# Graph network kernel: dot attention's edge one-hots made during propagation instead of in its own slot loop

## Time and profile before

| | |
|---|---|
| median of 3 runs | 1626.44 us (1622.48 to 1628.04) |
| the profiled execution | 1627.73 us, span 1625.9 us |
| propagation | 324.6 to 859 us |
| slot loop of graph attention | 995 to 1210 us |
| slot loop of dot attention | 1249 to 1524 us |
| busy share of the span: PE, DVE, ACT, POOL | 76%, 77%, 34%, 23% |

### The profile page before, as it was taken

The page is one execution under the profiler, slowest core; times in us unless marked ns, Lnnn a source line. Parts: engine busy times, 40 slices in busy tenths (PEclk is TensorE's granted clock), DMA queues, the critical chain, the costliest instruction groups (busy, mean ns, idle before and its releaser), DMA issues. The chain is left out here.

```text
span 1625.9 us, 44876 instructions
## 1 busy us (share of the span) xinstructions
PE 1237.4 (76%) x18543; PEld 1174.0 (72%) x18544; DVE 1259.8 (77%) x2302; ACT 546.2 (34%) x1096; POOL 373.9 (23%) x211
## 2 busy tenths in 40 slices
PE   4767777399999999999994004888856888888468
PEld 3356767399899999999993004787755887888368
DVE  7888888766566565665667998999988999999733
ACT  0047777400000000000002873333335777777311
POOL 1400000000000000000001012888862665656300
PEclk6858777699999999999997556999997999999789
DMA  0012222375475565654563683555513444543293
GB/s 10 0 46 109 105 103 109 109 249 190 151 240 204 161 196 194 213 194 164 203 213 110 225 298 123 204 201 189 200 68 117 144 159 149 164 146 122 96 343 101
DMA packets 74936, 256.85 MB, mean 158 GB/s; under 512 B 17999, under 2 KB 19576, under 8 KB 74732
## 3 DMA queue, kind: packets, MB, share of 16 engines
q1 hardware_dynamic: 59996, 211.70, 38.6%
q10 hardware_dynamic: 14400, 40.97, 6.5%
q0 software_dynamic: 336, 1.20, 0.3%
HBM read 168.15 MB, written 85.68 MB: 156 GB/s over the span
## 5 line engine op out<-in xcount | busy, mean ns | idle before, releaser
L1248 PE MATMUL psum<-work,count 128*128 128x192 f16 x6250 | 521.4, 247 | 30.7 <-issue 30.7
L1248 PEld LDWEIGHTS psum<-work,count 128*128 128x128 f16 x6250 | 519.7, 98 | 32.5 <-issue 31.8
L1171 DVE SCALAR_TENSOR_TENSOR work<-psum,small,work 128x96 f32<-128x96 f32 x250 | 79.5, 318 | 177.4 <-PE psum L1248 177.3
L1585 PE MATMUL psum<-count 128*128 128x98 f16 x625 | 113.1, 209 | 134.5 <-DVE count L1632 98.2
L1852 PE MATMUL psum<-count 128*128 128x100 f16 (+1 forms) x1875 | 181.4, 207 | 44.5 <-DVE count L1941 30.7
L1852 PEld LDWEIGHTS psum<-count 128*128 128x128 f16 x1875 | 162.7, 98 | 55.3 <-issue 36.0
L929 ACT ACTIVATE work<-work 128x1248 f32<-128x1248 f32 (+1 forms) x6 | 7.2, 1203 | 576.9 <-DVE work L912 576.8
L1917 POOL TENSOR_TENSOR count<-count 128x1000 bf16<-128x1000 f32 (+1 forms) x75 | 160.8, 2143 | 122.0 <-ACT count L1901 122.0
L1624 POOL TENSOR_TENSOR count<-count 128x970 bf16<-128x970 f32 (+1 forms) x75 | 166.7, 2236 | 91.2 <-ACT count L1617 91.2
L1853 PE MATMUL psum<-count 128*128 128x100 f16 (+1 forms) x1875 | 180.8, 207 | 0.0
L1853 PEld LDWEIGHTS psum<-count 128*128 128x128 f16 x1875 | 164.4, 98 | 0.0
(11 more groups left out here) (286 smaller groups left out, 2695.7 us busy)
## 6 DMA issues: line engine op xcount, KB each, us to landing
x<-bucket_rows_by_src SPq DMA_DIRECT2D x100, 400.0 KB, 4.6
onehots_by_src<-x ACTq DMA_DIRECT2D x100, 400.0 KB, 4.3
count<-bucket_rows_by_dst SPq DMA_DIRECT2D x50, 800.0 KB, 4.4
count<-onehots_by_src SPq DMA_DIRECT2D x50, 800.0 KB, 4.3
count_f<-count SPq DMA_DIRECT2D x25, 800.0 KB, 6.8
count<-count_turned SPq DMA_DIRECT2D x25, 800.0 KB, 5.8
count<-count_f SPq DMA_DIRECT2D x17, 800.0 KB, 4.3
count_turned<-x SPq DMA_DIRECT2D x25, 416.0 KB, 2.4
```

The source lines that it names most:

```text
L1248: last = nc.tensor.matmul(bank[i % BANKS], count16[:, j, i * P:(i + 1) * P], y[par][:, j, :], start=(j == 0), stop=(j == TILES - 1))
L1585: nc.tensor.matmul(ps[:, at:at + GW], node_hot[SRC][t % 2][:, s, :], high[:, s, :], start=True, stop=False, skip_group_check=True)
```

## The change

The edge one-hots of dot attention too are made in propagation and stored as a third set of 25 rows in hot_by_src. The 50 node rows are cut into 200 quarters of 800 columns with four buffers, the 25 edge rows into 125 fifths of 640 columns with two buffers. DVE compares one quarter after each of the tiles 1 to 20 of a step, and behind five quarters of every eight an edge fifth. The ids for the edge compares come from ids_dram in five chunks of five src tiles, 20 bytes for each partition and dst tile, into two buffers; two are loaded ahead of the first quarter, one each behind the loads of quarters 43, 83 and 123. POOL makes the iota. ACT's queue stores 325 pieces. The slot loop has no edge compare, loads three ready one-hot rows a tile, and the table `cols` is gone. To have semaphores for this, those of building are cleared and released. The code for further rounds follows suit. In the diff, `...` marks what is left out.

```diff
...
+    m["build_done"] = [prep, pe_prep, hist_hot, totals_done, spotted, prefixed, ranked, window_ready, window_used, slots_ready, ids_taken]
...
-HALF_ROW = NPAD // 2
-
-
-class NodeSpots:
...
-    def loads(self, sp, halves, row, n, beside=None):
-        for i in range(n):
-            if i >= 3:
-                sp.wait_ge(self.stored[i % 3], 16 * (i // 3))
-            sp.dma_start(halves[i % 3], row(i).broadcast_to([P, HALF_ROW])).then_inc(self.loaded[i % 3], 16)
...
-    def compare(self, dve, halves, i):
-        dve.wait_ge(self.loaded[i % 3], i // 3 * 16 + 16)
-        self.nc.vector.tensor_scalar(halves[i % 3], halves[i % 3], self.partition, None, ALU.is_equal).then_inc(self.spotted, 1)
...
+NODE_PIECE, EDGE_PIECE = NPAD // 4, 5 * P
+NODE_PIECES, EDGE_PIECES = 2 * TILES * 4, TILES * 5
+EDGE_AFTER = (0, 2, 3, 5, 7)
+NODE_BUFFERS, EDGE_BUFFERS, CHUNK = 4, 2, 5
+def edges_before(n):
+    return 5 * (n // 8) + sum(k < n % 8 for k in EDGE_AFTER)
+def made_with_edge(e):
+    return 8 * (e // 5) + EDGE_AFTER[e % 5] + 1 + e + 1
+class Spots:
...
+    def load_chunk(self, sp, pieces, k, c, ids_dram):
+        if c >= 2:
+            sp.wait_ge(self.made, made_with_edge((c - 1) * CHUNK * 5 - 1))
+        ids = ids_dram[bass.ds(k, 1)].rearrange("k p t n -> (k p) t n")[:, :, (SRC * TILES + c * CHUNK) * 2:(SRC * TILES + (c + 1) * CHUNK) * 2]
+        sp.dma_start(pieces.chunk[c % 2].rearrange("p t s d -> p t (s d)"), ids).then_inc(self.chunk_loaded[c % 2], 16)
+
+    def load(self, sp, pieces, k, n, ids_dram, by_src):
+        if n == 0:
+            for c in range(2):
+                self.load_chunk(sp, pieces, k, c, ids_dram)
+        if n >= NODE_BUFFERS:
+            sp.wait_ge(self.stored[n % NODE_BUFFERS], 16 * (n // NODE_BUFFERS))
+        w, part = divmod(n, 4)
+        row = by_src[bass.ds(k, 1), w].rearrange("k t n -> k (t n)")[:, part * NODE_PIECE:(part + 1) * NODE_PIECE]
+        sp.dma_start(pieces.node[n % NODE_BUFFERS], row.broadcast_to([P, NODE_PIECE])).then_inc(self.loaded[n % NODE_BUFFERS], 16)
+        c, rest = divmod(edges_before(n), CHUNK * 5)
+        if n % 8 in EDGE_AFTER and rest == 2 and 1 <= c < TILES // CHUNK - 1:
+            self.load_chunk(sp, pieces, k, c + 1, ids_dram)
+
+    def compare(self, dve, pieces, n):
+        dve.wait_ge(self.loaded[n % NODE_BUFFERS], 16 * (n // NODE_BUFFERS + 1))
+        self.nc.vector.tensor_scalar(pieces.node[n % NODE_BUFFERS], pieces.node[n % NODE_BUFFERS], self.partition, None, ALU.is_equal).then_inc(self.made, 1)
+        if n % 8 in EDGE_AFTER:
+            self.compare_edges(dve, pieces, edges_before(n))
+
+    def compare_edges(self, dve, pieces, e):
+        s, part = divmod(e, 5)
+        c = s // CHUNK
+        if e == 0:
+            dve.wait_ge(self.counted, 1)
+        if e >= EDGE_BUFFERS:
+            dve.wait_ge(self.edges_stored[e % EDGE_BUFFERS], 16 * (e // EDGE_BUFFERS))
+        dve.wait_ge(self.chunk_loaded[c % 2], 16 * (c // 2 + 1))
+        shape = [P, 5, P // 2, 2]
+        self.nc.vector.tensor_tensor(pieces.edge[e % EDGE_BUFFERS].rearrange("p (t n d) -> p t n d", n=P // 2, d=2),
+                                     pieces.iota.rearrange("p (n d) -> p n d", d=2).unsqueeze(1).broadcast_to(shape),
+                                     pieces.chunk[c % 2][:, part * 5:part * 5 + 5, s % CHUNK, :].unsqueeze(2).broadcast_to(shape), ALU.is_equal).then_inc(self.made, 1)
+
+    def stores(self, act, pieces, hot_by_src):
+        for n in range(NODE_PIECES):
+            act.wait_ge(self.made, n + 1 + edges_before(n))
...
+            if n % 8 in EDGE_AFTER:
+                e = edges_before(n)
+                act.wait_ge(self.made, made_with_edge(e))
+                s, part = divmod(e, 5)
+                act.dma_start(hot_by_src[:, 2 * TILES + s, part * EDGE_PIECE:(part + 1) * EDGE_PIECE], pieces.edge[e % EDGE_BUFFERS]).then_inc(self.edges_stored[e % EDGE_BUFFERS], 16)
...
     with nc.Block() as block:
+        @block.gpsimd
+        def _(pool):
+            clear_semaphores(nc, m["build_done"])
...
-            spots.loads(sp, halves, half_row, HALVES, store_count_tile)
+            for n in range(NODE_PIECES):
+                spots.load(sp, pieces, 0, n, ids_dram, by_src)
+                store_count_tile(n)
...
-            spots.wait_stored(pool, HALVES)
+            nc.gpsimd.iota(pieces.iota, [[1, P]], base=0, channel_multiplier=0, allow_small_or_imprecise_dtypes=True).then_inc(spots.counted, 1)
+            spots.wait_stored(pool)
             nc.gpsimd.memset(x[:, TILES - 1, :], 0.0).then_inc(x_free, 1)
...
-                        if i in SPOT_AFTER:
-                            spots.compare(dve, halves, turn * len(SPOT_AFTER) + SPOT_AFTER.index(i))
+                        if 1 <= i <= PIECES_A_STEP:
+                            spots.compare(dve, pieces, turn * PIECES_A_STEP + i - 1)
...
     def first_loads(sp, k):
         for s in range(3):
-            for v in (SRC, DST):
+            for v in (SRC, DST, EDGE):
                 load_hot(sp, s, v)
-            if s == 0:
-                load_cols(sp, k)
...
                 for s in range(3, TILES):
-                    for v, done in ((SRC, "q_done"), (DST, "v_done")):
+                    for v, done in ((SRC, "q_done"), (DST, "v_done"), (EDGE, "scattered")):
                         sp.wait_ge(S[done], (s - 2) * PER)
                         load_hot(sp, s, v)
...
-                            pe.wait_ge(S["edge_hot"], s + 1)
+                            pe.wait_ge(S["hot_%d%d" % (EDGE, s % 3)], 16 * (s // 3 + 1))
...
-                def spot_edges(s):
...
-                spot_edges(0)
...
-                        if s + 1 < TILES:
-                            if t0 == GROUP:
-                                spot_edges(s + 1)
...
-    hot_by_src = nc.dram_tensor("onehots_by_src", [P, 2 * TILES, NPAD], F16, kind="Internal").ap()
+    hot_by_src = nc.dram_tensor("onehots_by_src", [P, 3 * TILES, NPAD], F16, kind="Internal").ap()
```

More of the change, by code:

```diff
@@ L933, in _, with spot_next_round @@
             scalar_after(act)
-def spot_next_round(nc, m, halves, row, hot, n):
+def spot_next_round(nc, m, pieces, k, ids_dram, by_src, hot_by_src):
     spots = m["spots"]
@@ L941, in _, with many @@
         def _(sp):
-            if_one(sp, m, None, lambda: spots.loads(sp, halves, row, n))
+            def many():
+                for n in range(NODE_PIECES):
+                    spots.load(sp, pieces, k, n, ids_dram, by_src)
+            if_one(sp, m, None, many)
         @block.vector
@@ L946, in many @@
             def many():
-                for i in range(n):
-                    spots.compare(dve, halves, i)
+                dve.sem_inc(spots.counted, 1)
+                for n in range(NODE_PIECES):
+                    spots.compare(dve, pieces, n)
             if_one(dve, m, None, many)
@@ L953, in many @@
             def many():
-                spots.stores(act, halves, hot, n)
-                spots.wait_stored(act, n)
+                spots.stores(act, pieces, hot_by_src)
+                spots.wait_stored(act)
             if_one(act, m, None, many)
@@ new lines, in wait_stored, with __init__ @@
+    def wait_stored(self, eng):
+        for b in range(NODE_BUFFERS):
+            eng.wait_ge(self.stored[b], 16 * len(range(b, NODE_PIECES, NODE_BUFFERS)))
+        for b in range(EDGE_BUFFERS):
+            eng.wait_ge(self.edges_stored[b], 16 * len(range(b, EDGE_PIECES, EDGE_BUFFERS)))
+class Pieces:
+    def __init__(self, node, edge, chunk, iota):
+        self.node, self.edge, self.iota = node, edge, iota
+        self.chunk = [v.rearrange("p (t s d) -> p t s d", s=CHUNK, d=2) for v in chunk]
@@ L1155, in propagate @@
     rest = Residual(nc, m, cnt_dram, "step")
[L1156 to L1165, removed]
+    spots, idle = m["spots"], Space(m["x"])
+    node_pieces, edge_pieces = [idle.take(NODE_PIECE, F16) for _ in range(NODE_BUFFERS)], [idle.take(EDGE_PIECE, F16) for _ in range(EDGE_BUFFERS)]
+    chunks = [idle.take(2 * TILES * CHUNK, F16), view(m["work"], 4 * TILES * D + P, 2 * TILES * CHUNK, F16)]
+    pieces = Pieces(node_pieces, edge_pieces, chunks, view(m["small"], 160, P, F16))
+    PIECES_A_STEP = NODE_PIECES // K_STEPS
     def update(dve, n, from_bank, tile_of, y_next):
@@ L1217, in _ @@
         def _(act):
-            spots.stores(act, halves, half_hot, HALVES)
+            spots.stores(act, pieces, hot_by_src)
         @block.tensor
@@ L1255, in large @@
             def large():
-                for i in range(HALVES):
-                    spots.compare(dve, halves, i)
+                for n in range(NODE_PIECES):
+                    spots.compare(dve, pieces, n)
                 with dve.Fori(0, K_STEPS // 2) as kk:
@@ L1962, in dot_attention @@
         end_round(nc, [*S.values(), *m["spots"].all()])
-        spot_next_round(nc, m, halves, lambda i: by_src_half(by_src, k + 1, i), lambda i: hot_half(hot_by_src, i), BY_SRC_HALVES)
```

(1 more changed line is left out.)

67 lines of the change are left out of this document (28 added, 39 removed).

## The result

The changed kernel takes 1641.35 us (1638.7 to 1647.4, 6 runs) against 1627.24 for the kernel before in the same rounds: ratio 1.0087, interval 1.0064 to 1.0109. The forecast was 1603.5. The profiled execution has a span of 1645.6 us, 19.7 more than before; it is the slowest of the six (1647.4 us), so its parts add up to more than the 14.1 us between the medians.

| stretch | before | after | difference |
|---|---|---|---|
| up to the first product of propagation | 324.6 | 326.1 | +1.4 |
| first to last product of propagation | 533.8 | 569.0 | +35.2 |
| last product to DVE's multiply that waits for x | 2.5 | 10.9 | +8.4 |
| slot loop of dot attention, first to last multiply | 265.2 | 237.9 | -27.3 |
| all else | | | +2.0 |

The account below looks back on a forecast made before the run. It took DVE as full in the slot loop and PE as setting the pace in propagation. -29.3 + 0 + 4.4 + 2.0 = -22.9 from 1627.73 gave 1604.8, as median 1603.5; 8 in 10 range 1595 to 1618.

Parts of the forecast that it names:

- The ring of pieces: Propagation: a quarter's compare, store and load take about 6.7 us of the 8.3 four buffers leave, so 0 us.
- C: Rival, propagation: ring at the halves' medians, 9.3 us, PE waits 1.2 at each of ten step ends, 1615.5; chance 0.07.
- D: Slower rival, propagation: ring with both queues crowded; loss from a ring of 9.6 us, at 10.0 +44, 1647; chance 0.07.
- The slot loop: Dot attention: removing the edge compare gains 1.22 us in each of 24 tiles, -29.3 us.
- B: Rival, slot loop: DVE gets the full 1.73 us a tile, -41.5 + 6.4, 1591; chance 0.06.
- A: Rival: chunks of ids at 10 us, 1613.5, or PE's order leaving 0.7 us a tile, 1616; chance 0.18.
- DVE in propagation: Propagation: 61 us more DVE work, 1.85 us for a tile with both compares, hidden under PE's 2.07: 0 us.
- The first piece: Start of propagation: two id chunks of 5.0 us each delay the first quarter to 343.1, PE waits +4.4 us.
- the forecast of a quarter without chunks: Start of propagation: the first quarter, before counting the chunks, lands 0.5 us earlier than piece 0 at 333.6.
- tile 2's update: Start of propagation: PE needs it for tile 7 at 340.7, it comes at 345.1, so PE waits 4.4 us.
- The end: End of propagation: last quarter follows tile 20's update, load of x issued at 854.9 instead of 852.89, +2.0 us (1.5 to 4).

Follow-up runs that it names:

- the quarters alone: Kernel before with only node one-hots in 200 quarters and four buffers, edge compares left in the slot loop: 1636.49 us, ratio 1.0066.
- the square: Four kernels' propagation: quarters with neither edge compares nor edge stores 535.4 us, with compares 546.2, with stores 556.7, with both (changed kernel) 569.0.
- small_edge_stores: Changed kernel with edge stores of 32 columns instead of 640, the slot loop loading an SRC node row instead of the edge row: 1619.06 us, ratio 0.9953.

## Why the prediction was wrong

**The step that failed is "The ring of pieces", and in it one term.** It put a quarter's store and load at 3.3 + 3.0 us, the ring at 6.7 us and the cost at 0. The terms do not even follow from their own rule: half of what is over the least landing time is 1.0 us of the store's 4.3 and 0.7 of the load's 4.6, which leaves 3.3 + 3.9 + 0.33 + 0.1 = 7.6 us. And the rule was too kind. Measured, the ring takes about 9.4 us in the changed kernel and 8.8 with the quarters alone, against 8.3 that a buffer has. Quarters without edges land in 3.9 us as a load and 3.8 as a store at the median, at the least in 2.9 and 1.9; halves took 4.6 and 4.3, at the least 3.2 and 2.3. Half the size saved 0.7 and 0.5 us, where the sum needed 2.6 in all, and the edge stores gave most of it back (4.4 and 4.2). Three buffers of 1600 columns held 4800, four of 800 hold 3200; when the landing time hardly depends on the size, it is the columns held that set the rate. That more buffers would mend it follows from this but was not run.

**What it cost.** Of the 42.6 us between the forecast for the profiled execution (-22.9) and the measured +19.7, 30.8 lie in propagation (35.2 where I had 4.4) and 6.4 at its end (8.4 where I had 2.0). In propagation they are mostly the step ends, where PE waits for updates that late quarters held up, and the slower products behind such waits.

**The rivals had the mechanism and not its price.** C took the halves' medians, a ring of 9.3 us, which was right, and PE waits of 12 us in all; D named where the sign turns, a ring of 9.6, and gave 44 us at 10.0. At 9.4 us the runs show 29 to 35 us in propagation, PE's longer waits being 17 to 21 of them and its slower products 12 to 14. Neither rival had the clock. Neither had the single late landings, up to 8 us, nor the compares that take up the time for making up (at most 10.8 us by the square); both let DVE make up 3.8 us in tiles 21 to 24. The end was in neither: a late ring also delays the last stores. The waits of only 2.7 us before, my argument against D, spoke of three halves with 12.4 us to come round, not of this ring. I gave the two 0.14 together.

**The slot loop: right.** Forecast -29.3, measured -27.3 and in the kernel with nothing else changed 26 to 27 in time. The tile read from the last one before is there in every tile: from one to the next it is 9.62 us instead of 10.82, with 0.3 more in three of them, and the first two had been 0.17 shorter before. B is refuted by the wait of 0.39; that PE's order might halve the gain, one part of A, is refuted by PE's 221.7 busy us in 237.9 and by the gain itself. DMA at 78% was high, 61.4% by the queue's row for 66 loads, and the landing time rose from 4.3 to 6.0 us without anyone waiting, as the lead of two tiles said.

**DVE in propagation: right in size, wrong as "0 us".** A quarter takes 423 ns and a fifth 484, so that with what overlaps the next instruction they cost 0.35 and 0.40 of the queue (forecast 0.33 and 0.40). DVE was not full. But the slack counted as free was what made up for late pieces: up to 10.8 us by the square.

**The first piece: forecast +4.4, too dear.** It was compared at 338.8, not 343.1:

```profile
332.64 0.26 DVE L1236 TENSOR_TENSOR work<-work 128x96 f16<-128x96 f32 x1
338.79 0.43 DVE L1075 TENSOR_SCALAR x<-x,small 128x800 f16<-128x800 f16 x1 [5.89 <-DMA x<-bucket_rows_by_src]
```

Propagation also began 1.4 us later, so against the forecast of a quarter without chunks (333.1) they delayed it by 338.8 - 1.4 - 333.1 = 4.3 us. Counted from the first product, the first compare comes 12.7 us after it, and in the kernel with the quarters alone 7.5: 5.2 us by this, 2.2 to 2.6 a chunk instead of 5.0. The time lies ahead of the quarter's issue: SP's queue is busy with the two chunks (L1058) for 6.2 us, and the quarter's load then lands 5.4 us after its own issue, as it does without them (5.6).

```profile
327.10 1.96 SPq L1058 DMA_DIRECT2D x<-bucket_ids  x1
329.11 4.22 SPq L1058 DMA_DIRECT2D work<-bucket_ids  x1
333.37 10.80 SPq L1068 DMA_DIRECT2D x<-bucket_rows_by_src  x6
```

PE did not wait for tile 2's update; what step 0 lost came from late quarters further on. The rule of the Trainium skill, DMA: Bandwidth & Descriptors, section "Specifications", that transfers below 512 bytes are read, modified and written, would have doubled the price as the prediction supposed; 2.2 to 2.6 us for 200 runs an engine is 11 to 13 ns a run and shows nothing of the kind for loads into SBUF. The same page's section "Anatomy of one DMA", with a fixed part of about 2.0 us, gives a quarter 84% of a half's time (2.47 of 2.94). That fit was measured on GpSimd's queue; the transfers here go by SP's and ACT's. The medians without edges say 85% and 88%, which agrees with it. What lies above the fit, the part that the prediction put down to queues, was 1.7 and 1.4 us for halves and is 1.4 and 1.3 for quarters: it hardly went with the size either, by this estimate. That ratio, taken instead of the halved queues, would have given 3.8 + 3.6 + 0.4 = 7.9 us before any edge store, an estimate: too close to 8.3 to be called free.

**The end: +8.4 instead of +2.0.** The queue and DVE there:

```profile
893.90 0.49 DVE L1088 TENSOR_TENSOR x<-small,x 128x640 f16<-128x640 f16 x1
...
898.60 0.26 DVE L1236 TENSOR_TENSOR work<-work 128x96 f16<-128x96 f32 x1
905.95 2.66 DVE L1343 TENSOR_TENSOR work<-work,small 128x2400 f32<-128x2400 f32 x1 [7.10 <-DMA x<-in_x_dram]
```

```profile
898.28 0.78 SPq L1266 DMA_DIRECT2D x<-in_x_dram  x1
```

The last compare ends at 894.4, when PE is at its last product (895.0) instead of four tiles ahead of the end; its store lands at 897.8, the load of x is issued at 898.3, and DVE can start 7.7 us after that. Before, that load took 8.0 us (852.9 to 860.9), 5.5 of them beside PE's last tiles.

## What to carry to other kernels

A ring of buffers between DMAs has a rate of its own: columns in all buffers over the time of one round, and the round is made of landing times that shrank little with the piece here (4.6 to 3.9 us for half the size). Before pieces are cut smaller, count the bytes on the way and compare the time that each buffer has, not only the mean, with the medians as they are, then with the longest landings; the engine's spare time is what makes up for these, so other work put into it is not free. How the pieces are dealt over the loop may be worth more than their size: one line, four tiles of five instead of 20 in a row, was worth 21 us here.

## What the runs showed that was not expected

Landing times did not follow the size: 160 KB edge stores took 4.6 us at the median where 200 KB stores took 4.2, and 8 KB stores in small_edge_stores 4.0. Each edge store is issued right behind a quarter's store on ACT's queue, and no run tells whether it waits for that one or for the traffic.

PE's granted clock falls after its longer waits. Before, the waits at the ends of pairs of steps are 2.4 to 3.6 us, and the clock falls behind the first and the last of them, twice in propagation; in the changed kernel they are 4.6 to 5.2 us, and the clock falls behind all four, for longer, and twice behind the waits at the ends of single steps:

```profile
428.00:440.00 12.00, 8.38 (x83) 7.88 (x81) 3.65 (x14) 0.00 (x0) 0.00 (x0) 0.86 0.07 22
```

```profile
440.00:450.00 10.00, 5.09 (x40) 4.65 (x38) 4.49 (x18) 0.00 (x0) 0.00 (x0) 0.74 0.63 172
446.00:450.50 4.50, 4.50 (x29) 4.25 (x30) 0.29 (x1) 0.00 (x0) 0.00 (x0) 0.50 0.73 102
```

In the last of these rows, after a wait of 4.9 us, PE works without a pause at a granted clock of 0.50, the lower of its two levels (1.2 of 2.4 GHz). In all of propagation it stands there for 37 us instead of 10, and the products take 13.9 us longer. So a wait of PE here costs more than its length.

Two profiles of the same changed kernel differ by 6 us in propagation (569.0 and 562.8); the executions took 1647.4 and 1639.8 us, while the medians of the two sets of runs are the same (1641.35 and 1641.29).
